# A gated cross-attention and expert kernel on one core: three moves in VectorE's order, and one gate instruction folded into two others

## The reference, cut to what matters

```python
q, k, v = xn @ Wq + bq, y @ Wk + bk, y @ Wv + bv     # xn = layernorm(x); 16 heads of 16
attn = softmax(q k^T / 4);  h = relu((attn v) @ W1 + b1)
x1 = x + tanh(g_xattn) * (h @ W2 + b2)

xn2 = layernorm(x1)
scores = maximum(xn2 @ gate_W + gate_b, 1e-4)        # 8 experts
p = softmax(scores);  top 2 experts by p
w = maximum(p, 0.1), divided by the sum of the two chosen w, 0 for the others
out = x1 + tanh(g_ffn) * sum_e w_e * (xn2 @ expert_W[e] + expert_b[e]) / 2
```

## Time and profile before

| | before |
|---|---|
| median of three runs | 991.95 us (987.53 to 992.25) |
| profiled execution | 988.13 us |
| its span, first to last instruction | 986.4 us |
| mean granted TensorE clock | 0.976 |
| TensorE (PE) busy | 931.3 us, 94% of the span |
| VectorE (DVE) busy | 854.7 us, 87% |
| ScalarE (ACT) busy | 720.2 us, 73% |
| GpSimd (POOL) busy | 642.4 us, 65% |
| chain that ended last | PE 78%, DVE 10%, ACT 5%, issue 5% |

### The profile page before, as it was taken

One profiled execution on the slowest core, in us unless ns is written; L12 is line 12 of the kernel. 1 busy time (PEld: TensorE's weight loads), 2 busy tenths in 40 slices (PEclk: granted clock), 3 DMA queues, 4 the chain that ended last, 5 costly groups with the idle time before them and its releaser, 6 DMA issues.

```text
span 986.4 us, 26160 instructions
## 1 busy us (share of the span) xinstructions
PE 931.3 (94%) x9410; PEld 670.0 (68%) x9410; DVE 854.7 (87%) x2139; ACT 720.2 (73%) x1517; POOL 642.4 (65%) x792
## 2 busy tenths in 40 slices
PE   3679999999999999999999999999999999999987
PEld 2557777767776776776677677667767677777763
DVE  5787888988989888898898889889888988988875
ACT  4756878777787877777787777778777778777661
POOL 5445666667776567776666777666677766667743
PEclk8579999999999999999999999999999999999999
DMA  6000000000000000000000000000000000000000
GB/s 199 27 15 11 15 15 26 26 25 22 26 15 15 25 26 25 24 15 25 15 25 25 25 23 15 25 15 27 25 26 22 16 14 26 25 12 12 13 12 22
DMA packets 17471, 24.61 MB, mean 25 GB/s; under 512 B 2798, under 2 KB 8896, under 8 KB 17344
## 3 DMA queue, kind: packets, MB, share of 16 engines
q1 hardware_dynamic: 17344, 22.94, 7.4%
HBM read 14.54 MB, written 8.39 MB: 23 GB/s over the span
## 4 chain that ended last, share of the span: by engine, by line
PE 78%; DVE 10%; ACT 5%; issue 5%; POOL 1%; DMA 0%; POOLq 0%; ACTq 0%; DVEq 0%
PE e L740 28%; PE g L740 18%; PE t L923 9%; PE t L789 4%; PE g L940 3%; PE s L874 3%; PE s L811 2%; PE s L810 2%; PE s L809 2%; DVE row_max L1256 2%; PE g L749 2%; ACT p_f L557 2%; DVE acc L1211 2%; DVE p_lo L1194 2%; ACT p_hi L558 2%
## 5 line engine op out<-in xcount | busy, mean ns | idle before, releaser
L373 POOL TENSOR_TENSOR p_lo<-p_f,p_hi 77x512 f16<-77x512 f32 x160 | 184.4, 1168 | 221.5 <-ACT p_hi L558 221.5
L740 PE MATMUL e<-we_hi,x2T_lo 128*128 128x512 f16 x496 | 188.5, 380 | 4.8 <-DVE acc L1211 4.6
L740 PE MATMUL e<-we_hi,x2T_hi 128*128 128x512 f16 x496 | 187.8, 379 | 0.0
L740 PE MATMUL e<-we_lo,x2T_hi 128*128 128x512 f16 x496 | 187.8, 379 | 0.0
L557 ACT ACTIVATE p_f<-t 77x512 f32<-77x512 f32 x256 | 152.6, 596 | 27.5 <-PE t L789 25.0
L1211 DVE SCALAR_TENSOR_TENSOR acc<-e,comb,acc 128x256 f32<-128x256 f32 x307 | 146.2, 476 | 13.8 <-PE e L740 11.5
L558 ACT ACTIVATE p_hi<-t 77x512 f16<-77x512 f32 x256 | 152.6, 596 | 0.0
L1256 DVE TENSOR_REDUCE row_max<-s 128x6 f32<-128x462 f32 (+1 forms) x192 | 108.6, 579 | 19.8 <-PE s L874 19.2
L809 PE MATMUL s<-v_hi,p_lo 77*128 77x17 f16 x1024 | 98.3, 172 | 9.1 <-DVE p_lo L1194 6.1
L809 PEld LDWEIGHTS s<-v_hi,p_lo 77*128 77x128 f16 x1024 | 84.0, 96 | 29.5 <-issue 10.6
L636 ACT ACTIVATE scaled<-e,comb 128x256 f32<-128x256 f32 x126 | 56.4, 475 | 65.2 <-PE e L740 65.2
(11 more groups left out here) (194 smaller groups left out, 2881.0 us busy)
## 6 DMA issues: line engine op xcount, KB each, us to landing
x_sb<-in_x SPq DMA_DIRECT2D x32, 256.0 KB, 2.6
out<-acc SPq DMA_DIRECT2D x32, 256.0 KB, 2.0
we_f<-in_L_ffn_expert_W SPq DMA_DIRECT2D x2, 1024.0 KB, 9.5
y_sb<-in_ctx SPq DMA_DIRECT2D x32, 57.8 KB
w_f<-in_L_xattn_W SPq DMA_DIRECT2D x2, 512.0 KB, 7.4
wq_f<-in_L_xattn_Wq SPq DMA_DIRECT2D x1, 256.0 KB, 4.1
wkv_f<-in_L_xattn_Wk SPq DMA_DIRECT2D x1, 192.0 KB, 2.9
wkv_f<-in_L_xattn_Wv SPq DMA_DIRECT2D x1, 192.0 KB, 3.9
```

Source lines behind the costliest of these rows:

```text
L373: pool.tensor_tensor(p_lo[:, r].rearrange("m h n -> m (h n)"), p_f[:, r, :], p_hi[:, r].rearrange("m h n -> m (h n)"), ALU.subtract).then_ ...
L740: mm = pe.matmul(out_ap, a, c, start=(first and i == 0), stop=(last and i == n - 1))
```

## The change

- The list of VectorE has `yT_low(b)` ahead of `p_low(m, 0)`, where it was behind it.
- The list has `add_expert(f, 7, 1)` ahead of `take_max(b, 0)`, where it was behind it.
- Gate instruction 2 (`gs = max(graw, 1e-4)`) is gone. `graw` has a ninth column that GpSimd fills once with 1e-4, so the reduction over nine columns gives the floored maximum; the subtraction becomes a `scalar_tensor_tensor` that takes the maximum with 1e-4 and subtracts `gm1`. The differences of instruction 5 (now 4) are taken from `gshift` in place of `gs`. The gate has 12 instructions, and `p_low(m, 2)` stands behind the subtraction as before.

```diff
@@ -45,14 +45,14 @@
 
 MAX_CHUNKS = [[(0, 6)], [(6, 2), (8, 4)], [(12, 4)]]
 EARLY = 7 + 5
-CONSTS = EARLY + 1 + 7
+CONSTS = EARLY + 1 + 8
 PARTS = 4
 POOL_LOW = (1, 3, 4, 5, 6)
 VECTOR_LOW = (0, 2, 7)
 QUAD = 32
 SCALED = (2, 3)
 ADDED = [i for i in range(PAIRS) if i not in SCALED]
-GATE_OPS = 13
+GATE_OPS = 12
 EXPONENT = 0x7F800000
 SMALLEST = 2.0 ** -100
 HEADROOM = 2.0 ** 10
@@ -146,8 +146,9 @@
         ve2, rstd2 = sb("ve2", [P, T]), sb("rstd2", [P, T])
         xn2 = sb("xn2", [P, T, D])
         x2T_hi, x2T_lo = sb("x2T_hi", [P, 2, KC, N], F16), sb("x2T_lo", [P, 2, KC, N], F16)
-        graw, gs, gshift, gexp, gcount, gfloor, gw = (
-            sb(n, [P, T, E]) for n in ("graw", "gs", "gshift", "gexp", "gcount", "gfloor", "gw"))
+        graw = sb("graw", [P, T, E + 1])
+        gshift, gexp, gcount, gfloor, gw = (
+            sb(n, [P, T, E]) for n in ("gshift", "gexp", "gcount", "gfloor", "gw"))
         gdiff, gbeat = sb("gdiff", [P, T, E, E]), sb("gbeat", [P, T, E, E])
         gm1, gsum, gtot, grt = (sb(n, [P, T]) for n in ("gm1", "gsum", "gtot", "grt"))
         comb = sb("comb", [P, 2, T, E])
@@ -441,6 +442,7 @@
 
             pool.memset(v_hi[:, :, :, DH:DV], 1.0).then_inc(consts_ready, 1)
             pool.memset(v_lo[:, :, :, DH:DV], 0.0).then_inc(consts_ready, 1)
+            pool.memset(graw[:, :, E:E + 1], EPS).then_inc(consts_ready, 1)
             pool.wait_ge(consts_ready, CONSTS)
 
             def step(pair, u, s):
@@ -637,7 +639,7 @@
                                    scale=comb[:, u, t, 2 * c + j:2 * c + j + 1]).then_inc(expert_scaled, 1)
 
             def gate_exps(b):
-                act.wait_ge(gate_op, GATE_OPS * b + 4)
+                act.wait_ge(gate_op, GATE_OPS * b + 3)
                 act.activation(gexp[:], gshift[:], ACT.Exp).then_inc(gate_exp, 1)
 
             def step(pair, u, s):
@@ -1323,42 +1325,41 @@
 
                 if k == 1:
                     dve.wait_ge(gate_in_psum, b + 1)
-                elif k == 8:
+                elif k == 7:
                     dve.wait_ge(gate_exp, b + 1)
                 elif k == GATE_OPS:
                     dve.wait_ge(w_top_done, 6)
                 at_least(dve, gate_op, GATE_OPS * b + k - 1)
 
                 if k == 1:
-                    ins = dve.scalar_tensor_tensor(out=graw[:], in0=G_GATE[:, 0:T * E].rearrange("p (t e) -> p t e", t=T),
+                    ins = dve.scalar_tensor_tensor(out=graw[:, :, 0:E], in0=G_GATE[:, 0:T * E].rearrange("p (t e) -> p t e", t=T),
                                                    scalar=w_unscale[:, 1:2], in1=gb_rows[:].unsqueeze(1).to_broadcast([P, T, E]),
                                                    op0=ALU.mult, op1=ALU.add)
                 elif k == 2:
-                    ins = dve.tensor_scalar(gs[:], graw[:], EPS, None, ALU.max)
+                    ins = dve.tensor_reduce(gm1[:], graw[:], AX.X, ALU.max)
                 elif k == 3:
-                    ins = dve.tensor_reduce(gm1[:], gs[:], AX.X, ALU.max)
+                    ins = dve.scalar_tensor_tensor(out=gshift[:], in0=graw[:, :, 0:E], scalar=EPS, in1=wide(gm1),
+                                                   op0=ALU.max, op1=ALU.subtract)
+
                 elif k == 4:
-                    ins = dve.tensor_tensor(gshift[:], gs[:], wide(gm1), ALU.subtract)
-
+                    ins = dve.tensor_tensor(gdiff[:], gshift[:].unsqueeze(2).to_broadcast([P, T, E, E]),
+                                            gshift[:].unsqueeze(3).to_broadcast([P, T, E, E]), ALU.subtract)
                 elif k == 5:
-                    ins = dve.tensor_tensor(gdiff[:], gs[:].unsqueeze(2).to_broadcast([P, T, E, E]),
-                                            gs[:].unsqueeze(3).to_broadcast([P, T, E, E]), ALU.subtract)
+                    ins = dve.tensor_tensor(gbeat[:], gdiff[:], beat_from[:], ALU.is_gt)
                 elif k == 6:
-                    ins = dve.tensor_tensor(gbeat[:], gdiff[:], beat_from[:], ALU.is_gt)
+                    ins = dve.tensor_reduce(gcount[:], gbeat[:], AX.X, ALU.add)
+
                 elif k == 7:
-                    ins = dve.tensor_reduce(gcount[:], gbeat[:], AX.X, ALU.add)
-
+                    ins = dve.tensor_reduce(gsum[:], gexp[:], AX.X, ALU.add)
                 elif k == 8:
-                    ins = dve.tensor_reduce(gsum[:], gexp[:], AX.X, ALU.add)
-                elif k == 9:
                     ins = dve.scalar_tensor_tensor(out=gfloor[:], in0=wide(gsum), scalar=W_THRES, in1=gexp[:],
                                                    op0=ALU.mult, op1=ALU.max)
-                elif k == 10:
+                elif k == 9:
                     ins = dve.scalar_tensor_tensor(out=gw[:], in0=gcount[:], scalar=TOP_K - 0.5, in1=gfloor[:],
                                                    op0=ALU.is_lt, op1=ALU.mult)
+                elif k == 10:
+                    ins = dve.tensor_reduce(gtot[:], gw[:], AX.X, ALU.add)
                 elif k == 11:
-                    ins = dve.tensor_reduce(gtot[:], gw[:], AX.X, ALU.add)
-                elif k == 12:
                     ins = dve.reciprocal(grt[:], gtot[:])
                 else:
                     ins = dve.scalar_tensor_tensor(out=comb[:, u], in0=gw[:], scalar=ffn_scale[:, 0:1], in1=wide(grt),
@@ -1377,10 +1378,10 @@
                     key_value_weights_low()
                 if front:
                     xnT_low(b)
+                if front:
+                    yT_low(b)
                 if mid:
                     p_low(m, 0)
-                if front:
-                    yT_low(b)
                 if first:
                     gate(e, eu, 1)
                 if s == 0:
@@ -1390,24 +1391,23 @@
                 if first:
                     gate(e, eu, 2)
                     gate(e, eu, 3)
+                if mid:
+                    p_low(m, 2)
+                if first:
                     gate(e, eu, 4)
-                if mid:
-                    p_low(m, 2)
-                if first:
                     gate(e, eu, 5)
                     gate(e, eu, 6)
-                    gate(e, eu, 7)
                 if front:
                     kv_with_bias(b)
                 if s == 1:
                     experts_low(1)
                 if first:
+                    gate(e, eu, 7)
                     gate(e, eu, 8)
+                if front:
+                    q_with_bias(b)
+                if first:
                     gate(e, eu, 9)
-                if front:
-                    q_with_bias(b)
-                if first:
-                    gate(e, eu, 10)
                 if front:
                     q_high(b)
                 if s == 0:
@@ -1419,15 +1419,15 @@
                 if s == 1:
                     experts_low(2)
                 if first:
+                    gate(e, eu, 10)
+                if last:
+                    add_expert(f_pair, f, fu, 5, 0, s - 3)
+                if first:
                     gate(e, eu, 11)
                 if last:
-                    add_expert(f_pair, f, fu, 5, 0, s - 3)
+                    add_expert(f_pair, f, fu, 5, 1, s - 3)
                 if first:
                     gate(e, eu, 12)
-                if last:
-                    add_expert(f_pair, f, fu, 5, 1, s - 3)
-                if first:
-                    gate(e, eu, 13)
                 if last:
                     add_expert(f_pair, f, fu, 6, 0, s - 3)
                 if last:
@@ -1443,10 +1443,10 @@
                     normalise(m, 1, 1)
                 if last:
                     add_expert(f_pair, f, fu, 7, 0, s - 3)
-                if front:
-                    take_max(b, 0)
                 if last:
                     add_expert(f_pair, f, fu, 7, 1, s - 3)
+                if front:
+                    take_max(b, 0)
                 if mid:
                     oT_low(m)
                 if s == 0:
```

More of the change, by code:

```diff
@@ L1392, in step @@
                     gate(e, eu, 3)
-                    gate(e, eu, 4)
                 if mid:
@@ L1396, in step @@
                 if first:
+                    gate(e, eu, 4)
                     gate(e, eu, 5)
                     gate(e, eu, 6)
-                    gate(e, eu, 7)
                 if front:
@@ L1404, in step @@
                 if first:
+                    gate(e, eu, 7)
                     gate(e, eu, 8)
-                    gate(e, eu, 9)
                 if front:
@@ L1409, in step @@
                 if first:
-                    gate(e, eu, 10)
+                    gate(e, eu, 9)
                 if front:
@@ L1421, in step @@
                 if first:
-                    gate(e, eu, 11)
+                    gate(e, eu, 10)
                 if last:
@@ L1425, in step @@
                 if first:
-                    gate(e, eu, 12)
+                    gate(e, eu, 11)
                 if last:
@@ L1429, in step @@
                 if first:
-                    gate(e, eu, 13)
```

(5 more changed lines are left out.)

## The result

The changed kernel takes 976.49 us (median of four runs, 974.14 to 977.29) against 989.87 us for the kernel before (median of four, 987.53 to 992.25). The ratio is 0.9858, 95% interval 0.9833 to 0.9883. The profiled execution took 977.29 us with a span of 975.6 us; forecast were 976.5 us for a profiled execution and 980.3 us for the median. Most of the 3.8 us between the latter and 976.49 was the allowance for the median, which the changed kernel doesn't show: its profiled execution is the slowest of its four, and a fourth run of the kernel before brought that median down to 989.9. Among the experiments, one execution each of `e1_yt_only` and `e13_all_ordered` took about 3115 us and is left out of the medians and ratios.

The account below looks back on a forecast made before the run. TensorE's work plus its stops was taken as the bound: 988.1 - 11.4 - 0.0 - 0.2 = 976.5 us profiled, plus 3.8 us for a median of 980.3 us. Own range 977 to 984; 8 in 10, 971 to 988.

Parts of the forecast that it names:

- the allowance for the median: Whole kernel: 3.8 us added because the profiled execution lay that far under the median of the three runs.
- Part 1: `yT_low` ahead of `p_low(m, 0)`: TensorE's key product starts 0.38 us earlier in 30 steps, 11.4 us, between 4.8 and 12.3.
- Part 2: Last accumulation ahead of first maximum: expert 1's stop goes, 9.0 us on paper, zero booked because `mlp_down` waits for `h_lo`.
- both stops pay: Rival at `mlp_down`: `h_lo` follows TensorE by the whole amount, 9.0 us more go, 971.3 us; chance 0.17.
- Part 3: Gate's floor merged: worth 0 where GpSimd's `p_lo` lies over it, 0.2 us once in the last gate; bounds 0 and 5.8.
- the cover of the swap: Gate on VectorE: standing behind GpSimd's `p_lo`, about 0.8 us each at `gshift` and `gfloor`, hides the swap's 0.19 us.
- The slower rival: VectorE waits for a late `yT_hi` with `p_low` behind it: 0.19 us a step, 6.1 us, 998.0 us; chance 0.05.
- the second rival: In the attention, TensorE meets something that does not move; half of the first gain lost, 5.7 us, 986.0 us; chance 0.18.

Follow-up runs that it names:

- e1_yt_only: Kernel before with only `yT_low` moved ahead of `p_low(m, 0)`; 1035.13 us, ratio 1.0448.
- e13_all_ordered: e9 with a forced order, GpSimd's `key_blocks` 0 waiting for VectorE's `p_low` 7; 961.5 us, ratio 0.9726.
- e8: Changed kernel with `take_max(b, 0)` ahead of `add_expert(f, 7, 1)` again, so `yT_low` swap and merged floor only; 975.06 us, ratio 0.9848.
- e2: Kernel before with only `add_expert(f, 7, 1)` moved ahead of `take_max(b, 0)`; 990.28 us, ratio 0.9998.
- e4: Changed kernel with GpSimd's `add_biases`, `v_parts` and `x_with_bias` moved behind the scales of the second norm; 968.38 us, ratio 0.9786.
- e9: e4 plus a GpSimd wait for the second half of `xn2` ahead of the moved `add_biases`; 958.24 us, ratio 0.9676.
- e3: Changed kernel with both swaps undone, so only the gate's floor is merged; 987.08 us, ratio 0.9966.
- e14: Kernel before with only the `yT_low` swap, plus a memset of an unused tile in GpSimd's set-up; 1033.35 us, ratio 1.0441.
- e10: Changed kernel with an extra `tensor_scalar` maximum, SBUF to SBUF, where the gate's `gs` stood; 979.59 us, ratio 0.9886.
- e11: Kernel before with only the `yT_low` swap, plus GpSimd waiting for VectorE's `p_low` 7 ahead of `key_blocks` 0; 983.43 us, ratio 0.9939.
- e12: Changed kernel with VectorE's `p_low` 7 made to wait for GpSimd's `key_blocks` 0 of the same step; 1021.32 us, ratio 1.0323.
- e7: Changed kernel with an extra `tensor_reduce` into a spare tile where the gate's `gs` stood; 976.91 us, ratio 0.9856.

## Why the prediction was right, and where it was wrong

**Part 1, 0.38 us a step.** Measured 0.39 in the change and in e8. The distance from start to start was the right measure; the idle time of 0.16 us in the profile would have given less than half. ACT, POOL and DVE followed PE as described, seen in `gfloor`: 0.58 us instead of 0.97. The 0.38 was booked for the swap alone, though, and alone it loses (part 3).

**Part 2, nothing.** e2 and e8 show it from both sides. The gain was handed back at the last quarter of `mlp_down`, where 0.05 us between the end of `h_lo` and PE's start had told that PE was being released there already. e4 and e9 show that it was POOL's work over the `h_lo`: with that moved away, the step falls by 0.26 us and, with the lock taken off `xn2` too, by 0.47 in all. The rival "both stops pay" fell with this.

**Part 3, "worth 0".** This is the step that failed. As a term of the sum in the steady step it was right: e3 has 28.76 us. But I wrote that the cover of the swap was the standing time behind POOL and that without it 0.19 us would count, and priced the three parts one by one. The merge is not an extra to the swap, it is what makes the swap possible. Without it the swap costs 45 us, through a place 7 us further on that my text does not name: `p_low` 7 against `k_block`. The slower rival had the sign and the 0.19 us of delay, but the wrong place and 6 us instead of 45. One reading was too narrow as well: the prediction says that an instruction with both inputs in SBUF stands, but `gs` reads one tile of SBUF and stood for 0.94 of its 1.12 us in e1. The forecast of the whole came out because the change contains the merge, not because I had seen the danger.

**Luck in the total.** The 977.29 us of the profiled execution lie 0.8 us from the forecast partly by luck. Two things that the sum doesn't have nearly cancelled: the two long steps that went (3.4 us) and the late start (4.0 us). The median of 976.49 lies 0.5 us under the forecast's own range of 977 to 984, because of the allowance of 3.8 us. In the chances, half of the second rival is 0.09 and not 0.10, which changes nothing.

**The expected signs.** All came: no wait for `yT_lo` or `acc`, `gshift` at 0.90 us, the first `h_lo` of a step at 0.93 us (the pair at 1.46), a stop of 0.28 us at `mlp_down` (0.40 less 0.12), steps of 28.4 us.

**What stays open.** What makes POOL go first at `p_low` 7 in e1 and e14, and DVE in the steady steps of nearly all other kernels. The traces show a sign of it, the time at which ScalarE delivers `khT` (under the hardware), but no run moves that alone. The standing `gs` alone doesn't decide it: e10 has it and loses one step only, though with the smallest margin of all. Whether both swaps without the merge would lose it too was not run.

## What to carry to other kernels

Read stops from start to start, and look for places where an operand ends 0.05 us ahead of its user with no idle time booked: here the next gain was handed back there. Where VectorE and GpSimd both work on SBUF, their order is part of the schedule, and moving an instruction by 0.2 us can change it elsewhere; so price parts of a change together, run them apart, and look for instructions whose duration doubled. Moving GpSimd's long, non-urgent work off VectorE's urgent two-input instructions was worth more here (18 us) than the change itself (13 us).

## What the runs showed of the hardware

**Recorded order does not say who gets the ports; the operand's arrival goes with it.** Where `p_low` 7 (DVE) and `k_block` (POOL) both stand behind POOL's last `p_lo`, DVE's instruction is recorded as started 0.15 to 0.16 us ahead of POOL's, in the steady steps of every kernel without a forced order (the late ones of the next paragraph aside). In e10 DVE goes first (0.74 us, and POOL's `k_block` takes 1.70), in e1 POOL does (1.97 us and 1.25). The Trainium skill, "SBUF — State Buffer", section "Who interferes with whom", says that the order of issue decides who blocks. The trace agrees where one of the two is already running (`gs` took 0.18 us when issued 0.11 us ahead of POOL's `p_lo`, 1.12 us when 0.08 us behind), but between two that stand the recorded starts don't tell it.

What does differ is ScalarE's `khT`, the operand that `k_block` waits for: in e1 it ends at 451.97, 0.12 us ahead of the recorded start of `p_low` 7 at 452.09; in e10 it ends with that start, at 428.98 (ACT of e1, then ACT and POOL of e10):

```profile
451.68 0.29 ACT L588 ACTIVATE khT<-g 128x154 f16<-128x154 f16 x1
```

```profile
428.69 0.29 ACT L592 ACTIVATE khT<-g 128x154 f16<-128x154 f16 x1
...
429.13 1.70 POOL L429 TENSOR_TENSOR k_block<-own_head,khT 128x616 f16<-128x616 f16 x1
```

It is so in all 311 such meetings in the profiles of the eleven kernels without a forced order: `khT` ends up to 0.06 us behind the start of `p_low` 7 in the 256 in which DVE went first, and 0.10 to 0.12 us ahead of it in the 55 in which POOL did. In e10 the margin is under 0.02 us, and in its one lost step `khT` was 0.12 us ahead. This fits POOL being first in line when its operand is there before DVE issues, but it is an agreement of records and not an experiment. It doesn't cover the start either: in step 2 `khT` ends 0.15 us behind in all eleven, and DVE went first in eight, POOL in three (the changed kernel, e4, e14).

**Coming 0.09 us late costs 1.7 us.** The long steps of the kernel before show it. `comb` normally starts 0.07 us ahead of POOL's fifth `p_lo` and takes 0.23 us; in these two steps, 10 and 26, it came 0.02 us behind it, stood, and the step was 1.7 us longer. `comb` is late in the same two steps in e1, e2, e11, e12 and e14 (in e12 the step is no longer for it), and in none of the other kernels; what makes it late isn't known (timelines of the kernel before, DVE then POOL):

```profile
312.38 1.17 DVE L1364 SCALAR_TENSOR_TENSOR comb<-gw,ffn_scale,grt 128x16 f32<-128x16 f32 x1
...
314.38 0.90 DVE L1194 TENSOR_TENSOR p_lo<-p_f,p_hi 77x512 f16<-77x512 f32 x1
```

```profile
311.23 2.29 POOL L373 TENSOR_TENSOR p_lo<-p_f,p_hi 77x512 f16<-77x512 f32 x2 [0.21 <-ACT p_hi L558]
```

**The start scatters by about 3 us.** Step 2 took 31.9 us in the profile of the kernel before, 34.8 in the changed one, 31.5 in e8, 34.1 in e7 and 34.2 in e3, though their edits move nothing in it by that much. The busy times by stretch have the granted clock (the value after the busy times) at 0.88 for the kernel before and 0.76 for the changed one from 70 to 105 us:

```profile
70.00:105.00 35.00, 32.30 (x306) 23.31 (x305) 25.85 (x68) 25.61 (x55) 16.45 (x22) 0.88 0.04 13
```

```profile
70.00:105.00 35.00, 31.59 (x279) 23.15 (x278) 23.63 (x59) 22.22 (x48) 15.55 (x21) 0.76 0.03 10
```

The first is the kernel before, the second the changed one. In the same stretch e8 has 0.87, e7 and e3 have 0.76, so the long steps 2 go with the lower mean clock; which of the two brings the other isn't shown. The lost race (`p_low` 7 at 2.35 us) can only be a small part of the 2.9 us: e7 and e3 have 0.92 us there and are 0.6 to 0.8 us shorter. What moves the clock's rise was not tested.
